# Turning an expert's gathered rows on TensorE instead of in the DMA, in an attention and mixture-of-experts kernel

## The reference

```python
xn = _layernorm(x, axis=-1)
s = _L0_attn_ref(xn, norm_g, Wq, Wkv, Wout, out_norm_g)        # normalised q and k, softmax, Wout, layer norm
g = _silu(_L0_ffn_ref(xn, wr, w1, b1, w2, b2))
return x + s * g

# in _L0_ffn_ref
vals, idx = jax.lax.top_k(logits, TOP_K)                        # TOP_K = 2
cap = max(8, int(max(1, T * TOP_K // E) * CAP_FACTOR))          # 8192 * 2 // 8 * 1.25 = 2560
xg = x_pad[dispatch]                                            # (8, 2560, 256)
h = _gelu(jnp.einsum('ecd,edf->ecf', xg, w1) + b1[:, None, :])  # F = 1024
y = jnp.einsum('ecf,efd->ecd', h, w2) + b2[:, None, :]
wy = y * g[..., None]
out = jax.ops.segment_sum(wy.reshape(-1, D), dispatch.reshape(-1), num_segments=T + 1)[:T]
```

## Time and profile before

| | |
|---|---|
| median of 3 runs | 2854.68 us (2850.56 to 2862.34) |
| profiled execution | 2862.34 us, span 2860.6 us |
| TensorE busy | 2703.2 us, 94% |
| VectorE busy | 2048.4 us, 72% |
| ScalarE busy | 1829.0 us, 64% |
| GpSimd busy | 618.9 us, 22% |
| mean granted TensorE clock | 0.981 of 2.4 GHz |
| expert stage | first matmul 1069.84 us, last first-layer matmul about 1894 us |

### The profile page before, as it was taken

How to read it: one execution, slowest core, us unless ns; L and a number is a source line. 1 busy time by engine, 2 the same in 40 slices (tenths; PEclk the granted TensorE clock), 3 DMA queues, 4 the chain that set the end, 5 groups by cost and what they waited for, 6 DMA issues and landing times.

```text
span 2860.6 us, 84972 instructions
## 1 busy us (share of the span) xinstructions
PE 2703.2 (94%) x37573; PEld 1791.2 (63%) x37637; DVE 2048.4 (72%) x3077; ACT 1829.0 (64%) x2355; POOL 618.9 (22%) x428
## 2 busy tenths in 40 slices
PE   4999999998899989999999999999999999999996
PEld 3566666665566656666666676666666666666664
DVE  5788888888888874334333434338999989999996
ACT  6777777765676756455554545447777767777764
POOL 3111111110888310000000000002233333333212
PEclk8999999999999999999999999999999999999997
DMA  3223222100433101313222322210111111111101
GB/s 104 72 94 98 85 98 76 63 28 28 154 111 118 54 20 51 84 52 84 84 49 82 81 60 76 52 45 24 39 54 52 53 51 45 52 47 50 41 23 44
DMA packets 207649, 184.07 MB, mean 64 GB/s; under 512 B 99048, under 2 KB 185008, under 8 KB 207280
## 3 DMA queue, kind: packets, MB, share of 16 engines
q1 hardware_dynamic: 194992, 145.06, 17.2%
q0 software_dynamic: 12288, 33.57, 3.7%
HBM read 71.61 MB, written 85.98 MB: 55 GB/s over the span
## 4 chain that ended last, share of the span: by engine, by line
PE 73%; DVE 12%; ACT 7%; issue 6%; POOL 1%; DMA 1%; SPq 0%; DVEq 0%; POOLq 0%; ACTq 0%
PE pair L598 20%; PE bank L655 14%; PE pair L641 13%; PE bank L618 6%; PE bank L626 6%; PE bank L616 6%; DVE arena L1151 6%; ACT arena L807 2%; PE bank L537 2%; PE bank L579 2%; PE bank L549 1%; PE bank L506 1%; PE bank L567 1%; DVE qhl L1073 1%; ACT h_f L814 1%
## 5 line engine op out<-in xcount | busy, mean ns | idle before, releaser
L1151 DVE TENSOR_TENSOR arena<-arena 128x1024 bf16<-128x1024 f32 (+1 forms) x1032 | 1226.3, 1212 | 207.9 <-ACT arena L807 203.6
L807 ACT ACTIVATE arena<-pair 128x1024 f32<-128x1024 f32 (+1 forms) x1032 | 1014.3, 1017 | 317.5 <-PE pair L598 312.1
L598 PE MATMUL pair<-qT,kT 128*128 128x512 f16 (+1 forms) x4096 | 884.7, 386 | 24.8 <-ACT arena L807 21.7
L618 PE MATMUL bank<-vhl,arena 128*128 128x64 bf16 x8192 | 648.2, 195 | 0.0
L616 PE MATMUL bank<-vhl,arena 128*128 128x65 bf16 x8192 | 647.0, 193 | 0.9 <-DVE att L1144 0.8
L616 PEld LDWEIGHTS bank<-vhl,arena 128*128 128x128 bf16 x8192 | 566.9, 99 | 52.1 <-DVE att L1144 1.1
L618 PEld LDWEIGHTS bank<-vhl,arena 128*128 128x128 bf16 x8192 | 548.7, 97 | 51.7 <-issue 0.8
L598 PEld LDWEIGHTS pair<-qT,kT 128*128 128x128 f16 (+1 forms) x4096 | 200.5, 96 | 475.8 <-issue 419.0
L814 ACT ACTIVATE h_f<-pair,b1T 128x512 f32<-128x512 f32 x320 | 218.9, 684 | 381.5 <-PE pair L641 381.1
L1200 POOL TENSOR_TENSOR q_small<-q_small,minus_half 128x8 f32<-128x8 f32 x64 | 148.8, 2325 | 1395.6 <-DVE q_small L1064 1395.3
L655 PE MATMUL bank<-w_hl,arena 128*128 128x256 bf16 x3840 | 426.8, 273 | 0.4
(11 more groups left out here) (188 smaller groups left out, 1916.3 us busy)
## 6 DMA issues: line engine op xcount, KB each, us to landing
routed_rows<-h_f SPq DMA_DIRECT2D x80, 256.0 KB, 4.6
expert_rows<-att SPq DMA_DIRECT2D x40, 512.0 KB, 2.8
raw<-in_L_ffn_w SPq DMA_DIRECT2D x32, 512.0 KB
xn_rows<-s_hl SPq DMA_DIRECT2D x16, 512.0 KB, 2.9
xT_out<-xn_rows SPq DMA_DIRECT2D x64, 128.0 KB
w_lo<-in_L_attn_x SPq DMA_DIRECT2D x64, 128.0 KB
out<-w_lo SPq DMA_DIRECT2D x64, 128.0 KB
s_xin<-in_L_attn_x SPq DMA_DIRECT2D x12, 512.0 KB, 5.1
```

The costliest lines, as they stand in the source:

```text
L598: t = nc.tensor.matmul(into, kT[g // BG % 2][rows, part, keys], qT[g % 2][rows, h, :], start=(turn == 0), stop=(turn == 1))
L618: nc.tensor.matmul(bank[:, at:at + DH], p_top[:, s, cols, 1], V[:, kb, DH + 1:VW], start=False, stop=False, skip_group_check=True)
L807: nc.scalar.activation(p_f32[:, n % NP, columns(n)], pairs[n % 2][:, columns(n)], ACT.Exp).then_inc(exped, 1)
L1151: nc.vector.tensor_tensor(p_lo[:, n % NP, c], p_f32[:, n % NP, c], p_top[:, n % NP, c, 1], ALU.subtract).then_inc(lowed, 1)
```

## The change

The rows of a group are loaded as they lie (`xg`, one plain DMA of 512 KB, in the buffer `att[0]`), and TensorE turns them: 16 transposes of 128 x 128 into two PSUM banks, bank 3 by the ring and bank 2, each copied by ScalarE to `xgT`, which now lies in `kT[1]`. A new main slot, "turn", holds this. Turn 0 stands first in the stage; turn fg + 1 stands after hidden fg, ahead of second fg - 1. A partition now takes four rows that lie side by side in `routed_rows`, and `expert_rows` is written in the same order, 4 KB in a row. The slots of the projection of group 7 move: `O_AT` is one slot later at tile 28, and five slots apart where it was four.

```diff
     attention_slots(0, CUT)
-    experts_at = len(slots)
+    slots.append(("turn", 0, 0))
     for fg in range(FG + 1):
         if fg < FG:
             slots += [("hidden", fg, f) for f in range(FC)]
+        if fg + 1 < FG:
+            slots.append(("turn", fg + 1, 0))
         if fg:
             slots += [("second", fg - 1, j) for j in range(GT)]
...
+    experts_at = place["turn", 0, 0]
...
-            O_AT.append(experts_at + 4 * j)
+            O_AT.append(experts_at + 1 + 5 * j)
...
+        xg = [cut(flat(att[(XG + 1) % 2], F16), i, [GT, 2 * D]) for i in range(2)]
-        xgT = [cut(flat(att[(XG + 1) % 2], F16), i, [2 * DC, GP]) for i in range(2)]
+        xgT = [cut(flat(kT[1], F16), i, [2 * DC, GP]) for i in range(2)]
...
+            def turn_gathered(fg):
+                i = fg % 2
+                pe.wait_ge(x_gathered[i], 16 * (fg // 2 + 1))
+                for half in range(2):
+                    if half:
+                        bank = acc_banks[2][:, :]
+                        pe.wait_ge(divided, (XG + 1) * H)
+                        pe.wait_ge(xgT_copied, 2 * fg)
+                    else:
+                        bank, free = side.take(xgT_copied, 2 * fg + 1)
+                        pe.wait_ge(*free)
+                    where["xgT", fg, half] = bank
+                    view = bank.bitcast(F16)
+                    n = 0
+                    for k in range(2 * DC):
+                        for j in range(2):
+                            t = nc.tensor.transpose(view[:, n * P:(n + 1) * P],
+                                                    xg[i][:, 2 * half + j, k * P:(k + 1) * P], ident16[:, :])
+                            n += 1
+                    t.then_inc(xg_turned, 1)
...
-                pe.wait_ge(xgT_loaded[fg % 2], 16 * 2 * DC * (fg // 2 + 1))
+                pe.wait_ge(xgT_copied, 2 * (fg + 1))
...
+            def copy_turned(fg):
+                act.wait_ge(scored, CUT)
+                act.wait_ge(hidden, FC * (fg - 1))
+                for half in range(2):
+                    act.wait_ge(xg_turned, 2 * fg + half + 1)
+                    cast(xgT[fg % 2][:, :, half * 2 * P:(half + 1) * 2 * P],
+                         where["xgT", fg, half].bitcast(F16).rearrange("p (k c) -> p k c", k=2 * DC)
+                         ).then_inc(xgT_copied, 1)
...
-                sp.wait_ge(hidden, FC * (fg - 1))
-                for k in range(2 * DC):
-                    nc.sync.dma_start(xgT[fg % 2][:, k, :], routed_groups[fg, :, k * P:(k + 1) * P],
-                                      transpose=True).then_inc(xgT_loaded[fg % 2], 16)
+                sp.wait_ge(xg_turned, 2 * (fg - 1))
+                nc.sync.dma_start(xg[fg % 2], routed_tiles[e, :, q * GT:(q + 1) * GT, :]).then_inc(x_gathered[fg % 2], 16)
...
-                nc.sync.dma_start(expert_groups[fg], yout[fg % 2]
+                nc.sync.dma_start(expert_tiles[e, :, q * GT:(q + 1) * GT, :], yout[fg % 2]
```

More of the change, by code:

```diff
@@ L115, in build_program @@
     xn_tiles = xn_rows.rearrange("(t p) d -> t p d", p=P)
-    routed_groups = routed_rows[0:ROWS, :].rearrange("(f n) d -> f n d", n=GP)
-    expert_groups = expert_rows.rearrange("(f j p) d -> f p j d", j=GT, p=P)
+    routed_tiles = routed_rows[0:ROWS, :].rearrange("(e p j) d -> e p j d", p=P, j=CT)
+    expert_tiles = expert_rows.rearrange("(e p j) d -> e p j d", p=P, j=CT)
     attn_tiles = attn_rows.rearrange("(t p) d -> t p d", p=P)
@@ L365, in build_program @@
         b2_loaded = [sem(f"b2_loaded{i}") for i in range(2)]
-        xgT_loaded = [sem(f"xgT_loaded{i}") for i in range(2)]
-        hidden, gelued, h_cast, h_rest = [sem(n) for n in ("hidden", "gelued", "h_cast", "h_rest")]
+        x_gathered = [sem(f"x_gathered{i}") for i in range(2)]
+        xg_turned, xgT_copied, hidden, gelued, h_cast, h_rest = [sem(n) for n in (
+            "xg_turned", "xgT_copied", "hidden", "gelued", "h_cast", "h_rest")]
         expert_out, y_done = sem("expert_out"), sem("y_done")
@@ L606, in weigh @@
                     pe.wait_ge(y_done, FG * GT)
+                    pe.wait_ge(xgT_copied, 2 * FG)
                 for i, g, h, kb in halves(n):
@@ L672, in main @@
                         weigh(n)
+                elif kind == "turn":
+                    turn_gathered(a)
                 elif kind == "hidden":
@@ L754, in prepare_kv @@
                 act.wait_ge(scored, steps_to(BG * (b - 1) - 1) if b >= 2 else 0)
+                if b == 3:
+                    act.wait_ge(hidden, FG * FC)
                 cast(kT[b % 2][:, :, gi * GP:(gi + 1) * GP], where["kT", g].bitcast(F16).rearrange(
@@ L824, in main @@
                         exponent(a)
+                elif kind == "turn":
+                    copy_turned(a)
                 elif kind == "hidden":
@@ L1139, in divide @@
                     if g == XG + 1:
-                        dve.wait_ge(hidden, FG * FC)
+                        dve.wait_ge(xg_turned, 2 * FG)
                     if g == XG + 2:
@@ L1339, in load_routed @@
             def load_routed(fg):
+                e, q = divmod(fg, NQ)
                 yield from clock.at(max(SCATTER_AT + 2 * NT, O_AT[XG * GT - 1] + O_TURN[0]) + 8 if fg < 2 else
```

## The result

The changed kernel takes 2897.63 us (median of 4 runs, 2894.68 to 2901.12) and the kernel before 2854.83 (4 runs, 2850.56 to 2862.34). That is 42.8 us slower, a ratio of 1.0147 with a 95% interval of 1.0122 to 1.0172. I had forecast 2894 us in a range of 2880 to 2910.

The account below looks back on a forecast made before the run. TensorE was taken to bound the expert stage, with no slack. Turns 34.3, entry, copies and loads 0, and start 4.6 sum to 38.9 us, which on the 2854.7 median gives 2894 us, range 2880 to 2910.

Parts of the forecast that it names:

- The bound: Expert stage: TensorE busy 789.64 of 790.00 us, so work added to its queue lengthens the kernel one for one.
- 39 turns at 0.88 us, 34.3 us: Expert stage, turns 1 to 39: 16 transposes each at 0.055 us, in a queue without slack, add 34.3 us.
- The DMAs removed are worth nothing, apart from the entry: Expert stage: TensorE waited for the transposing DMAs once, 7.9 us at the entry, all that removing them can give directly.
- Entry, 0: Entry to the expert stage: plain load, turn and copies put the first matmul at 1069.7 against 1069.84; 0, ends -4 and +3.
- Start, +4.6: Groups 0 to 2: shared bank 3 and uncovered copies add 4.26 + 2.0 - 1.7 = +4.6 us, ends +2 and +9.
- Copies cost 0: Steady state: ScalarE's 80 copies, 82 us, are covered by the 10.4 us second layer; cost 0.
- Sum: Whole kernel: 34.3 + 0 + 4.6 = 38.9 us more, giving 2894 us on the median.
- Turns at half clock: Rival, expert stage: transposes don't hold the clock, 0.112 us each, 39 us more, 2930 us; chance 0.07.
- Exposed copies: Rival, steady state: next group's hidden waits 3 us for each turn's copies, 114 us, 3008 us; chance 0.03.
- Matmuls slowed by the DMAs: Part of the no-change rival, expert matmuls: transposing DMAs cause 1.3% wider spacing, 11 us back; about 2866 us, chance 0.06.

Follow-up runs that it names:

- before_loads_once: Kernel before, with only the loads of groups 0 and 1, so 38 of 40 groups multiply old rows: 2902.68 against 2900.60 us, ratio 1.0004.
- before_early: Kernel before, with group 0's four transposing DMAs early into xT_out: 2895.57 against 2901.17 us; run again, 2893.81 against 2902.46 us.
- own_bank: Changed kernel, with the first half of turns 0, 1 and 2 in bank 1 instead of bank 3: 2936.07 us; kernel before in that session 2901.17.
- copied_twice: Changed kernel, with each of ScalarE's two copies of turns 3 to 39 done twice: 2948.50 us; kernel before in that session 2900.60.
- turned_twice: Changed kernel, with the transposes of turns 3 to 39 issued twice, 592 more: 2974.51 us; kernel before in that session 2900.60.
- turned_eight: Changed kernel, with turns 3 to 39 issued eight times, 128 transposes in a row: 3128.59 us; kernel before in that session 2860.70.
- one_of_eight: Changed kernel, with 1 transpose of 8 in each half of turns 3 to 39, copies as large: 2914.50 us; kernel before in that session 2900.60.
- start_early: Changed kernel, with first halves of turns 0 to 2 in bank 1, turn 1 inside hidden 0, group 0 loaded early: 2930.68 us; kernel before 2901.17.

## Why the prediction was right, point by point

- *The bound.* TensorE had no slack in the expert stage, so its added work would show one for one. Shown: turns with 2, 16, 32 and 128 transposes give 0.056 us for each more.
- *39 turns at 0.88 us, 34.3 us.* Measured 0.89, 34.8 us. The rest, with 37 of them (33.0 us), grew by 32.4. Two small effects that the forecast did not have partly cancel there and make up the 0.6 us: six short waits for the bias addition in the kernel before, 0.22 us each from start to start, are gone, and the wait of 0.62 us at tile 31 is new.
- *The DMAs removed are worth nothing, apart from the entry.* Shown by before_loads_once (0.0 us in the rest). Shown too by before_early, which gets back the 7.9 us and the half clock; that is all that there was to gain on that side.
- *Entry, 0.* Measured +0.2. Turn 0 could start 4.3 us after the plain load was issued, the first layer of the kernel before 7.2 us after its first transposing DMA was, and turn and copies took 3.1 us (1060.49 to 1063.56), as worked out.
- *Start, +4.6.* Measured +8.4, of which 1.8 are turns 1 and 2 that I had counted with the turns: +6.6. The waits alone sum to 5.75 against 1.70 before, +4.1. The remaining 2.4 us is the clock, which fell at turn 1 behind the wait for s_rows. This is the one term that was mis-sized; I had it only as an upper end. It is no accident of one execution: the clock fell at turn 1 in all six traces of kernels that have this start. own_bank shows the cause: with the first gap away, the clock stayed, though the second gap was still there.
- *Copies cost 0.* True in the changed kernel, but with less room than I thought. I asked only when the first layer needs them, and put the limit at 11 us of work against 5. copied_twice shows the nearer limit, by the weight casts queued behind them, then VectorE, then a bank: 2 us more of copies already reach it.
- *Sum.* 38.9 forecast; the stage measured 41.0 in the traces, and the medians of two sessions differ by 40.5 and 42.8. The terms were right one by one, except for the clock at turn 1. Two figures of the working are off by a little: its ends (32 to 47 on 2850 to 2860) add up to 2882 to 2907, not 2884 to 2906, and at 0.112 us a transpose a turn costs 0.9 us more, not 1.0, which gives the 2930 that stands there.
- *Rivals.* Turns at half clock: ruled out by turned_twice and turned_eight. Exposed copies: ruled out for the rest; at turns 1 and 2 they cost nearly what the forecast had there (1.55 and 1.82 us against 1.8 and 2.0). Matmuls slowed by the DMAs: ruled out by before_loads_once.

## What to carry to other kernels

A transposing DMA that costs 1.26 us of a queue is cheaper than the four TensorE transposes of 0.056 us that replace it, when TensorE is the bound and the queue has time: price an operation where it is added, not alone. When a wait at the head of a stage is all that a change can win, look first at what makes the transfer late; here another buffer for the first group won it without touching the steady state. And before calling work on another engine free, ask what is queued behind it and who waits for that, not only for its own result.

## What had not been expected

- In the six traces with the changed kernel's start the clock fell at turn 1, behind an idle time of 2.4 us: in four of them while the transposes still ran, in two (turned_twice, one_of_eight) in the idle time behind them. In start_early it fell in the second of two idle times, 1.40 and 1.58 us, with 0.9 us of transposes between them. It held after 1.67 us alone (own_bank), after 1.82 us before a projection and after the 1.00 us of the earlier trace rows; a single 3.20 us lowered it. So the length of the last gap alone does not tell. What exactly decides was not tried.
- The same kernel before took 2855, 2901, 2901, 2902 and 2861 us in five sessions. Most of the difference lies in the first attention half, while the rows are scattered. In such a slower trace (before_loads_once) TensorE has small idle times there for which the profile names nothing but issue, 7.7, 6.7 and 4.6 us for the three lines that multiply the attention weights by the values (616, 618 and 626), and the clock is at 0.90 from 800 to 900 us instead of 1.00. The cause is open; it has no part in this change.
